# A twelve-sublayer decoder on one core: gathered cross-attention and a ternary feed-forward layer reordered

## The reference

```
x = x + L0_attn(norm(x));  x = x + L0_xattn(norm(x), ctx);  x = x + L0_ffn(norm(x))
x = x + L1_attn(norm(x));  x = x + L1_xattn(norm(x), ctx);  x = x + L1_ffn(norm(x))
x = x + L2_attn(norm(x));  x = x + L2_xattn(ctx, norm(x));  x = x + L2_ffn(norm(x))
x = x + L3_attn(norm(x));  x = x + L3_xattn(norm(x), ctx);  x = x + L3_ffn(norm(x))
```

```
L1_xattn:  Q, K, V = h Wq + bq, ctx Wk + bk, ctx Wv + bv        (16 heads of width 8)
           head i sees only the context rows i, i+16, i+32, ... (32 of 512)
           softmax(Q K^T / sqrt(8)) V, then Wo + bo
L3_ffn:    quant_weight(w): s = max(mean|w|, 1e-5);  clip(round(w / s), -1, 1) * s
           quant_act(x):    c = 127 / max(max|row|, 1e-5); clip(round(x c), -128, 127) / c
           g = gelu(quant_act(h) quant_weight(w1)^T)            (128 -> 512)
           quant_act(g) quant_weight(w2)^T                      (512 -> 128)
```

## Time and profile before

| | |
|---|---|
| three timed runs | 1631.58, 1636.93, 1637.21 us; median 1636.93 |
| profiled execution | 1631.73 us, span 1629.5 us, mean granted TensorE clock 0.859 |
| busy, share of the span | PE 76%, DVE 58%, ACT 42%, POOL 15% |
| L1_xattn, start of its norm to its last update of x | 460.8 to 534.05 us |
| L3_ffn, from h to its last update of x | 1564.9 to 1625.8 us |
| DMA | 114.55 MB, 70 GB/s over the span |

### The profile page before, as it was taken

How to read it: one execution, slowest core, us unless ns; L and a number is a source line. 1 busy time by engine, 2 the same in 40 slices (tenths; PEclk the granted TensorE clock), 3 DMA queues, 4 the chain that set the end, 5 groups by cost and what they waited for, 6 DMA issues and landing times. The chain is left out here.

```text
span 1629.5 us, 26020 instructions
## 1 busy us (share of the span) xinstructions
PE 1242.9 (76%) x9190; PEld 758.0 (47%) x9234; DVE 941.5 (58%) x2485; ACT 691.0 (42%) x1299; POOL 251.8 (15%) x525
## 2 busy tenths in 40 slices
PE   4777997784875487456999999999857689789922
PEld 1333434672331387234666666666547423323311
DVE  5558864335654444664676676767530555677666
ACT  2544872221622021101666666666424235446612
POOL 2211111451010254100000000000036112111100
PEclk8787998897896599767999999999968779989965
DMA  5425210784330366000000000000056331311000
GB/s 138 116 81 139 70 63 25 220 274 100 68 110 0 136 226 200 13 0 0 1 2 1 1 2 1 1 1 2 9 152 213 100 88 22 102 53 39 17 13 13
DMA packets 85553, 114.55 MB, mean 70 GB/s; under 512 B 11234, under 2 KB 65711, under 8 KB 85151
## 3 DMA queue, kind: packets, MB, share of 16 engines
q1 hardware_dynamic: 80978, 103.78, 21.8%
q0 software_dynamic: 4448, 9.12, 1.8%
HBM read 85.79 MB, written 26.61 MB: 69 GB/s over the span
## 5 line engine op out<-in xcount | busy, mean ns | idle before, releaser
L662 DVE TENSOR_REDUCE mx<-ps 128x4 f32<-128x1024 f32 (+1 forms) x128 | 153.7, 1222 | 72.0 <-PE ps L599 63.7
L805 PE MATMUL ps<-probs,vaug 128*32 128x256 f32 (+1 forms) x1792 | 145.8, 400 | 13.3 <-ACT probs L773 9.1
L2175 DVE CUSTOM_DVE_ANT_0 wring<-ps,probs 128x768 f32<-128x768 f32 x128 | 122.6, 958 | 56.9 <-PE ps L2047 56.8
L2131 ACT COPY qs<-ps 128x768 f32<-128x768 f32 x128 | 102.4, 801 | 97.6 <-PE ps L2054 97.6
L763 ACT ACTIVATE probs<-ps 128x1024 f32<-128x1024 f32 x96 | 98.3, 1024 | 86.1 <-PE ps L637 86.1
L768 ACT ACTIVATE probs<-ps 128x512 f32<-128x512 f32 x192 | 106.2, 594 | 51.3 <-PE ps L725 49.4
L2113 ACT ACTIVATE wring<-wring,r 128x768 f32<-128x768 f32 x128 | 120.7, 943 | 2.9 <-DVE r L2178 2.9
L236 POOL TENSOR_TENSOR rstd<-veps,mhalf 128x8 f32<-128x8 f32 x14 | 23.2, 1657 | 617.9 <-DVE veps L221 590.6
L599 PE MATMUL ps<-ks,qs 49*128 49x256 bf16 (+1 forms) x512 | 85.0, 374 | 39.6 <-DVE mx L657 12.0
L2054 PE MATMUL ps<-ident,wring 128*128 128x128 f32 x768 | 110.4, 281 | 3.2 <-DVE wring L2212 3.2
L2054 PEld LDWEIGHTS ps<-ident,wring 128*128 128x128 f32 x768 | 84.6, 141 | 39.4 <-issue 35.3
(11 more groups left out here) (313 smaller groups left out, 2352.4 us busy)
## 6 DMA issues: line engine op xcount, KB each, us to landing
wring<-in_L_ffn_w SPq DMA_DIRECT2D x19, 768.0 KB
wring<-in_L_ffn_w SPq DMA_DIRECT2D x32, 384.0 KB
wring<-in_L_ffn_w SPq DMA_DIRECT2D x19, 514.0 KB
scr_q<-probs SPq DMA_DIRECT2D x10, 384.0 KB, 3.4
scr_k<-probs SPq DMA_DIRECT2D x27, 128.0 KB, 4.2
qs<-scr_q SPq DMA_DIRECT2D x18, 192.0 KB
probs<-in_L_ffn_w SPq DMA_DIRECT2D x8, 384.0 KB
probs<-in_L_ffn_w SPq DMA_DIRECT2D x4, 768.0 KB
```

The lines of the kernel that those rows point to most:

```text
L662: dve.tensor_reduce(out, src, AX.X, ALU.max, negate=True).then_inc(a_max.sem, 1)
L805: ins = pe.matmul(ps[32 * j:32 * j + 32, self.av_bank(s), q0:S], vaug[:, s % 2, kt, j, :], probs[:, s % 2, j, at:at + S - q0], start=(kt = ...
L2131: act.copy(self.pT[:, g % 2, j, :, k * P:(k + 1) * P], self.buffer("turn", i, 0, KV).rearrange("p (t n) -> p t n", n=P)).then_inc(self.out ...
L2175: dve.tensor_tensor_reduce(self.sc[:, s, :], src, self.maskb[:, u // (2 * PR), :], 1.0, -3.0e38, ALU.add, ALU.max, self.top[:, s:s + 1]).t ...
```

## The change

In L1_xattn the context is loaded without a wait into the upper half of `qs`; PE makes the keys before the norm's transposes, in place of the dummy matmuls, and DVE masks two batches in the norm's hook and two after h. Queries come before values; the bias and mask of the values are applied after the scores of tile 1. `pr` has three buffers and `pT` two. PE issues score t+1 ahead of turn t-1, and the output products of a batch inside the loop, two batches behind. SP waits for the keys and values before it issues the six loads of L2_xattn.

In L3_ffn the weights are loaded at the start of L2_ffn, their magnitudes summed behind the copy of its block 5, the sum over partitions made at the start of L3_attn, the rounding done between L3_attn's projections and its loop. The scales of all 8 token tiles are computed together, the tiles quantised in two halves. ACT's Gelu reads PSUM and scales by a column, so L2346 is gone; the inner tiles are quantised in pairs with two slots, four products with w1 run ahead, and x is stored in four DMAs. ACT begins the sublayer with a Gelu of one column.

```diff
                     others[7].context_vector(dve, *divmod(b - 2, CTX_STEPS))
+                if m == 2 and b == 6:
+                    others[11].weights_vector(dve)
...
+        ctxg = qs[:, B * PAIRS * S + 1024:].bitcast(F32)[:, 0:TC]
+        pr = tmp[:, TC + 512 + T:TC + 2048 + T].rearrange("p (s n) -> p s n", s=3)
+        pT = tmp[:, TC + 2048 + T:TC + 2048 + 3 * T].rearrange("p (s c n) -> p s c n", s=2, c=NQ)
...
         def sync(self, sp):
-            sp.wait_ge(x_done.sem, x_done.at(self.sub - 1, 1))
             sp.dma_start(self.ctxg, a["ctxT_by_head"]).then_inc(g_ctx.sem, 16)
...
+        def context_tensor(self, pe):
             pe.wait_ge(g_ctx.sem, 16)
             for b in range(B):
                 pe.matmul(bank(b), wt("L1_xattn_k"), self.ctxg[:, b * S2:(b + 1) * S2],
                           start=True, stop=True).then_inc(g_k_mm.sem, 1)
+
+        def tensor(self, pe):
+            for c in range(2):
+                pe.wait_ge(ln_hT.sem, ln_hT.at(self.norm, c + 1))
+                pe.matmul(bank(5 + c), wt("L1_xattn_q"), hT[:, c * 512:c * 512 + 512],
+                          start=True, stop=True).then_inc(two_mm.sem, 1)
             for t in range(B * NQ):
                 c = t % NQ
                 ins = pe.matmul(bank(4, t * 32, t * 32 + 32), self.ctxg[:, t * P:(t + 1) * P],
                                 wt("L1_xattn_v")[:, c * 32:c * 32 + 32], start=True, stop=True)
             ins.then_inc(g_v_mm.sem, 1)
...
+            self.score_tensor(pe, 0)
+            for t in range(NT + 1):
+                if t + 1 < NT:
+                    self.score_tensor(pe, t + 1)
+                if t:
+                    self.turn_tensor(pe, t - 1)
+                if t and t % 2 == 0:
+                    self.sum_tensor(pe, t // 2 - 1)
+                if t >= 4 and t % 2 == 0:
+                    self.y_tensor(pe, t // 2 - 2)
+            self.y_tensor(pe, B - 1)
+
...
-                    act.activation(self.pr[:, t % 2, :], self.pr[:, t % 2, :], ACT.Exp).then_inc(tile_act.sem, 1)
+                    act.activation(self.pr[:, t % 3, :], self.pr[:, t % 3, :], ACT.Exp).then_inc(tile_act.sem, 1)
                 elif what == "turn":
                     act.wait_ge(tile_tp.sem, tile_tp.at(0, t + 1))
-                    if t >= 2 and t % 2 == 0:
-                        act.wait_ge(g_av.sem, g_av.at(0, t // 2))
...
+        def context_vector(self, dve):
+            self.keys_vector(dve, 0)
+            self.keys_vector(dve, 1)
+
+        def keys_vector(self, dve, b):
+            dve.wait_ge(g_k_mm.sem, g_k_mm.at(0, b + 1))
...
+            self.keys_vector(dve, 2)
+            self.keys_vector(dve, 3)
...
-                    if t >= 2:
-                        dve.wait_ge(tile_tp.sem, tile_tp.at(0, t - 1))
+                    if t >= 3:
+                        dve.wait_ge(tile_tp.sem, tile_tp.at(0, t - 2))
                     dve.tensor_tensor(pr, src, wide(top), ALU.subtract).then_inc(g_s_sub.sem, 1)
+                    if t == 1:
+                        self.values_vector(dve)
...
+        held = qs[:, B * PAIRS * S:].bitcast(F32)
...
         def sync(self, sp):
-            sp.wait_ge(x_done.sem, x_done.at(self.sub - 1, 1))
+            sp.wait_ge(x_done.sem, x_done.at(7, 1))
             sp.dma_start(self.w1, a["L3_ffn_w1"]).then_inc(f_in.sem, 16)
             sp.dma_start(self.w2, a["L3_ffn_w2"]).then_inc(f_in.sem, 16)
 
+        def out_sync(self, sp):
+            for p in range(NT // 2):
+                sp.wait_ge(f_done.sem, f_done.at(0, 2 * p + 2))
+                sp.dma_start(a["out"].rearrange("(t p) d -> p t d", p=P)[:, 2 * p:2 * p + 2, :],
+                             x[:, 2 * p:2 * p + 2, :]).then_inc(written, 16)
+
...
+        def weights_tensor(self, pe):
+
+            pe.wait_ge(f_abs.sem, f_abs.at(0, 1))
+            pe.matmul(bank(0, 0, 2), self.ones, self.col(0, 2), start=True, stop=True).then_inc(f_tot.sem, 1)
...
+            pe.wait_ge(f_wq.sem, f_wq.at(0, 2))
+            for t in range(4):
+                self.up_tensor(pe, t)
+            for p in range(NT // 2):
+                self.turn_tensor(pe, 2 * p)
+                self.turn_tensor(pe, 2 * p + 1)
+                if 2 * p + 4 < NT:
+                    self.up_tensor(pe, 2 * p + 4)
+                    self.up_tensor(pe, 2 * p + 5)
+                self.down_tensor(pe, 2 * p)
+                self.down_tensor(pe, 2 * p + 1)
+
...
+            act.activation(self.col(128), self.ones[:, 0:1], ACT.Gelu)
...
+            for t in range(4):
+                self.gelu_scalar(act, t)
+            for q in range(NT):
+                act.wait_ge(tile_tp.sem, tile_tp.at(1, q + 1))
+                if q >= 2:
+                    act.wait_ge(f_y.sem, f_y.at(0, q - 1))
+                act.copy(self.ziT[:, q % 2, :], bank(2 + q % 2).bitcast(BF16)[:, 0:FH]).then_inc(tile_T.sem, 1)
+                if q % 2 and q + 3 < NT:
+                    self.gelu_scalar(act, q + 3)
+                    self.gelu_scalar(act, q + 4)
+
+        def gelu_scalar(self, act, t):
+            act.wait_ge(f_h.sem, f_h.at(0, t + 1))
+            if t >= 4:
+                act.wait_ge(f_hq.sem, f_hq.at(0, t // 2 - 1))
+            act.activation(self.z[:, t // 2 % 2, t % 2, :], bank(self.h_bank[t % 4]), ACT.Gelu,
+                           scale=self.col(16 + t)).then_inc(tile_act.sem, 1)
+
...
+        def rounded_vector(self, dve):
+
             do = lambda ins: link(dve, dchain, ins)
...
+                do(dve.tensor_scalar(self.wtmp, wgt, self.col(4 + k), ROUND, ALU.mult, ALU.add))
                 do(dve.tensor_scalar(self.wtmp, self.wtmp, ROUND, 1.0, ALU.subtract, ALU.min))
                 dve.tensor_scalar(self.wint[:, k, :], self.wtmp, -1.0, None, ALU.max).then_inc(f_wq.sem, 1)
                 dve.wait_ge(f_wq.sem, f_wq.at(0, k + 1))
...
+        def scales_vector(self, dve, big, inv, scale, weight, n):
+
+            do = lambda ins: link(dve, dchain, ins)
+            do(dve.tensor_scalar(self.col(big, n), self.col(big, n), EPS, None, ALU.max))
+            do(dve.reciprocal(self.col(inv, n), self.col(big, n)))
+            do(dve.tensor_scalar(self.col(inv, n), self.col(inv, n), 127.0, None, ALU.mult))
+            do(dve.tensor_scalar(self.col(scale, n), self.col(big, n), 1.0 / 127.0, self.col(weight), ALU.mult, ALU.mult))
+
+        def hidden_vector(self, dve, p):
+            z, zi = self.z[:, p % 2, :, :], self.zi[:, p % 2, :, :]
+            dve.wait_ge(tile_act.sem, tile_act.at(1, 2 * p + 2))
+            link(dve, dchain, dve.tensor_reduce(self.col(48 + 2 * p, 2), z, AX.X, ALU.max, apply_absolute_value=True))
+            self.scales_vector(dve, 48 + 2 * p, 56 + 2 * p, 32 + 2 * p, 3, 2)
+            for t in range(2):
+                ins = dve.tensor_scalar(z[:, t, :], z[:, t, :], self.col(56 + 2 * p + t), ROUND, ALU.mult, ALU.add)
+            link(dve, dchain, ins)
+            if p >= 2:
+                dve.wait_ge(tile_tp.sem, tile_tp.at(1, 2 * p - 2))
+            dve.tensor_scalar(zi, z, ROUND, None, ALU.subtract).then_inc(f_hq.sem, 1)
+
...
+        def vector(self, dve):
+            dve.wait_ge(ln_h.sem, ln_h.at(made(self.norm), 1))
+            link(dve, dchain, dve.tensor_reduce(self.col(64, NT), h[:, :, :], AX.X, ALU.max, apply_absolute_value=True))
+            self.scales_vector(dve, 64, 72, 16, 2, NT)
+            for half in range(2):
+                tiles = range(4 * half, 4 * half + 4)
+                for t in tiles:
+                    ins = dve.tensor_scalar(h[:, t, :], h[:, t, :], self.col(72 + t), ROUND, ALU.mult, ALU.add)
+                link(dve, dchain, ins)
+                dve.tensor_scalar(self.hi[:, 4 * half:4 * half + 4, :], h[:, 4 * half:4 * half + 4, :], ROUND, None,
+                                  ALU.subtract).then_inc(f_q.sem, 1)
+            for p in range(NT // 2):
+                self.hidden_vector(dve, p)
+                if p:
+                    self.out_vector(dve, 2 * p - 2)
+                    self.out_vector(dve, 2 * p - 1)
+            self.out_vector(dve, NT - 2)
+            self.out_vector(dve, NT - 1)
...
+                if s == 8:
+                    others[11].sync(sp)
                 mixtures[s].sync(sp)
-            elif s in others and s != 7:
+            elif s in others and s not in (7, 11):
                 others[s].sync(sp)
                 if s == 4:
+                    sp.wait_ge(g_k_mm.sem, g_k_mm.at(0, B))
+                    sp.wait_ge(g_v_mm.sem, g_v_mm.at(0, 1))
                     others[7].sync(sp)
-        sp.wait_ge(x_done.sem, x_done.at(N_SUB_RUN - 1, 1))
-        sp.dma_start(a["out"].rearrange("(t p) d -> p t d", p=P), x[:, :, :]).then_inc(written, 16)
-        sp.wait_ge(written, 48)
+        others[11].out_sync(sp)
+        sp.wait_ge(written, 96)
...
-                norm_vector(dve, norm_of[s], meanwhile=subs[s].context_vector if s in subs and subs[s].cross else None)
```

(11 more changed lines are left out.)

249 lines of the change are left out of this document (98 added, 151 removed).

## The result

The changed kernel takes 1571.17 us (median of four runs, 1568.29 to 1576.57), the kernel before 1634.26 (median of four); the ratio is 0.9627, with a 95% interval of 0.9578 to 0.9676. The profiled execution took 1572.72 us, its span is 1570.6. The forecast was 1572.0 for that execution and 1575 for the median. So the total was hit closely, but terms of the sum missed in opposite ways, and the experiments are mostly about these.

What follows compares the result with a forecast made beforehand. Bound: the order of work in L1_xattn, DVE in L3_ffn. Savings 26.7 + 33.1 + 0.8 - 0.9 = 59.7 us gave 1572.0 for the profiled execution; 3 on top for the median made 1575, range 1567 to 1586.

Steps and rivals of the forecast that it cites:

- Part 1: L1_xattn's front: keys ahead of the norm and queries before values gain 4.1 us, first reduction at 475.3.
- Part 2: L1_xattn's loop, scores a tile ahead: sublayer ends at 507.3 instead of 534.05, gaining 26.7 us including the front.
- the walk through PE's queue: L1_xattn's loop: PE's steps behind an odd tile summed, giving a pair 8.8 us at the lower clock, 6.6 at full.
- I take 30% of the time at the lower: L1_xattn's loop and end: clock share chosen between 36.8 us (lower) and 30.0 (full); sublayer gain 26.7, between 22.0 and 28.8.
- Rival 1: L1_xattn's loop stays at the lower clock: 4.8 us more, 1580; chance 0.13.
- Rival 2: L1_xattn: scores ahead don't break the ring, ACT's or PE's order keeps pairs near 13.5 us: 1595; chance 0.05.
- Part 3: L3_ffn from h to the last update: 27.8 us instead of 60.9, 33.1 saved, DVE setting the pace.
- Rival 3: L3_ffn: the ring through PE and ACT sets the pace at 6 us a pair, not 4.4: 1581; chance 0.07.
- The stores: End of L3_ffn: output in four 128 KB stores instead of one saves 0.8 us, between -0.6 and 1.1.
- Costs elsewhere: Moved weight work: nothing in L2_ffn, 0.5 plus 0.4 us in L3_attn; bounds 0 and 3.
- The 0.5 for the tiny product on PE: L3_attn: a narrow product ahead of the dummy matmuls delays PE by 0.5 us, between 0 and 0.9.
- Rival 4: Slower than before: SP's new waits delay L2_xattn's six loads so DVE stands still in L1_ffn; chance 0.01.

Runs made afterwards that it cites:

- Experiment 3: Changed kernel with L1_xattn's key matmuls and masked copies behind the norm again: norm start to first reduction 17.25 us against 14.52; L1_xattn 49.7 us.
- experiments 1: Kernel before with only the change of L1_xattn, L3_ffn and its store as before: 1585.81 us, ratio 0.9824.
- 7: Changed kernel with both L3_ffn weights summed and rounded at the start of L3_ffn instead of earlier sublayers: L3_ffn 40.62 us instead of 35.46.
- 8: Changed kernel with the scale of each L3_ffn token tile worked out by itself: L3_ffn 43.64 us, 8.2 longer.
- 9: Changed kernel with one 512 KB store at the end instead of four: 3.7 us from last update of x to span end, against 2.26 to 2.37.
- 10: Changed kernel with the first three w1 products and their Gelus in L3_ffn ahead of the second four token tiles: L3_ffn 34.17 us, 1.3 less.
- experiment 4: Changed kernel with L1_xattn's scores of tile t+1 behind the transposes and sums of tile t-1 again: 1577.08 us, L1_xattn 71.31.
- the first and the third batch: First four and last four follow-up runs, on chips numbered 13 and 9; kernel before took 1612.69 and 1616.38 us there.
- the second batch: The middle four follow-up runs, on the chip numbered 13; kernel before took 1633.23 us there.

## Why the forecast was right, and where it was off

**Part 1.** Forecast 4.1, measured 4.05. The keys end 6.3 us behind the norm's start, not 5, and the transposes, which wait for h, hide that. Experiment 3 shows that the keys alone are worth 2.7 of it. So close a hit is in part luck: the forecast gave the front no spread by the clock, and with 14.3 to 15.8 us in eleven traces the gain was anywhere from 2.8 to 4.25.

**Part 2, the step that was mis-sized.** First reduction to the multiplication of tile 1: forecast 8.65, measured 8.6 to 9.0. Behind it the bounds of the walk through PE's queue hold up well, in eight traces with the same loop (the changed kernel twice, and experiments 1, 3, 7, 8, 9 and 10):

| stretch | forecast, full / lower | measured at clock 1.00 | measured lower (clock) |
|---|---|---|---|
| pair of tiles 2, 3 | 6.1 / 7.9 | 6.15 | 7.98 to 8.00 (0.50 to 0.67) |
| pair of tiles 4, 5 | 6.6 / 8.8 | 6.58 to 6.60 (one of them at 0.99) | 7.92 to 8.22 (0.78 to 0.79) |
| pair of tiles 6, 7 | 4.8 / 5.75 | 4.72 to 4.73 | 4.72 to 5.17 (0.67 to 0.73) |
| end | 3.8 / 5.65 | 4.01 to 4.02 | 4.52 to 5.72 (0.50 to 0.77) |
| loop and end | 30.0 / 36.8 | | 30.9 to 34.4, mean 33.2 (0.70 to 0.85) |

What failed is "I take 30% of the time at the lower": it made 32.0 us, and the profiled execution took 34.2, which by the same two ends is (34.2 - 30.0) / 6.8 = 62%. Nor does the time follow the share: the clock of 0.76 over loop and end means 48% at the lower level, and the pair of tiles 2 and 3 took 7.99 us at a clock of 0.50 and at 0.67 alike. In seven of the eight traces that pair met a low clock. So the sublayer saved 24.5 instead of 26.7, inside the 22.0 to 28.8 that I had given. Rival 1, the whole loop at the lower clock, didn't come: no trace shows it in all stretches. Nor is there one right share; the same loop gave 30.9 and 34.4 us. The Trainium skill (TensorE: Matmul & The Clock Gate, A second HAM failure mode) describes such swinging between half and full rate in groups of matmuls with small pauses; the traces agree that it swings, with 0.62, 0.79, 1.00 and 0.73 in four stretches that follow each other; that the pauses are the cause, no run here shows.

**Rival 2** (the ring isn't broken, 13.5 us a pair) fell, and experiment 4 shows that it would have been true for the other order.

**Part 3.** Forecast 27.8 us from h, measured 26.7, so 34.2 saved instead of 33.1. By steps: tokens quantised in 4.8 (5.15), first pair at 8.13 (8.5), a pair 3.65 (3.76), two updates 0.52 (0.65), the end 2.83 (2.95). Nearly every term was a little dear: the wide subtraction took 0.69 where I took 0.78 between 0.55 and 0.86, and four products 0.87 where I had 1.07. The wait ahead of the first pair came out at the 3.35 that I had added up, though the Gelus in it were dearer. What I misread is the loop before: I called DVE "nearly always at work" there, but 7.5 us of it were waits for PE's product with w2, one in each tile. The new order, in which the updates of a pair stand behind the next pair, has no wait there until the last two, 1.47 us. By the experiments 5.2 us of the 35.65 come from the moved weights (7), 8.2 from the gathered token tiles (8) and 1.4 from the stores (9). The other 20.9, the inner loop, rest on the timelines: no run takes its pairs, or the Gelu out of PSUM, back by itself. Rival 3 fell, as DVE has no idle time between the pairs. The Gelu with a column operand took 0.695 us, where the earlier trace rows had 0.63 from SBUF and the exponential at L768, which reads PSUM at the same width and without such an operand, 0.594. The group on ScalarE, and then the page's row of that exponential (busy us, mean ns):

```profile
L2366 ACT ACTIVATE probs<-ps,r 128x512 f32<-128x512 f32 x8 | 5.0, 695 | 0.7 <-PE ps L2323 0.7
```

```profile
L768 ACT ACTIVATE probs<-ps 128x512 f32<-128x512 f32 x192 | 106.2, 594 | 53.0 <-PE ps L725 51.1
```

So the difference is 0.10 here, of which the column is the likely but not the only possible cause, since the functions differ too. The Trainium skill (ScalarE: Activation LUTs, What ACT_TABLE_LOAD costs) gives 93 ns for a column; the traces agree with that.

**The stores** saved 1.4 us, not 0.8, and experiment 9 confirms it. I had forecast a tail of 2.8 us, from the 2.5 in which a 128 KB write landed; it was 2.3 us in all, with the issue in it, as SyncE's queue shows in the changed kernel (span end 1570.6):

```profile
1568.34 0.37 SPq L2285 DMA_DIRECT2D out<-x  x1
```

The Trainium skill (DMA: Bandwidth & Descriptors, Anatomy of one DMA) names some 2.0 us as the fixed part of a DMA. That section is about DMAs that GpSimd issues, and these stores are issued by SyncE; both tails measured here, 2.3 us for 128 KB and 3.7 for 512 KB, lie above it.

**Costs elsewhere.** I had put 0.9 on L3_attn. Its first maximum came 0.6 late, as worked out, but the third only 0.2, since another wait ends there. The 0.5 for the tiny product on PE didn't appear: behind the dummy matmuls PE now waits 1.35 us for h, where the earlier trace rows had 0.16. PE's timeline there:

```profile
1259.57 0.58 PE L2298 MATMUL ps<-r,qs 128*128 128x2 f32 x2 [7.28 <-DVEq L2550]
1260.01 4.71 PE L2580 MATMUL ps<-m3a,identb 128*128 128x512 bf16 x15
1266.08 1.09 PE L244 MATMUL ps<-ident,h 128*128 128x128 f32 x8 [1.35 <-DVE h L226]
```

The error was to take the 0.16 as a fixed margin. It goes with the clock of the dummies: they ended 6.35 us behind the norm's start at 0.54 in the kernel before, and 5.23 at 0.71 in the changed one. The transposes started 6.51 us behind the norm's start in the three traces without the product and 6.58 or 6.59 in the eleven with it, even in the one in which the dummies, at 0.55, ended no earlier than h. So product and means together cost 0.07 us there. L3_attn as a whole took 116.9 to 118.1 us in the three traces without the rounding and 117.4 to 118.7 in the eleven with it; what is left, some 0.5 us, is within its own spread. L2_ffn: nothing, as forecast. Rival 4 was far away: the six loads are issued from 472.39 to 477.14, and the first that reads them starts at 550.98. L1_ffn (122.99 and 123.10 us) and L2_xattn (419.35 and 419.49) didn't grow.

**The sum.** Against the profiled span before: 24.5 + 35.65 + 0.2 = 60.35 saved in the sublayers that I had costed at 59.7, and 1.4 us lost in all the others together, which leaves 58.9 (1629.5 to 1570.6). The loop's 2.2 us too few stand against 1.1 in L3_ffn, 0.6 in the stores and 1.1 in L3_attn. That the profiled execution came within 0.7 us of 1572.0 is luck: the misses cancel, and the first sublayer alone, which nothing touches, took from 110.6 to 117.4 us in the fourteen traces. The 3 us that I put on top for the median weren't needed; the median lies 1.5 below the profiled execution this time.

## What to carry to other kernels

Where two engines hand tiles to each other in a ring, look at what stands in the queue ahead of the operation that the other engine needs next: here putting that one first was worth over 20 us, and without it the further buffers gained nothing. Price such a loop at both clock levels and forecast the middle of them with the full width as its range (here 33.4 us, and eight traces had a mean of 33.2), unless the bound is an engine whose time didn't change with that clock. Before you call an engine the bound, add up its waits: DVE in L3_ffn looked always busy and waited 7.5 us. A vector instruction on one number per lane costs nearly what one on eight does (0.15 against 0.17 us here), so gather the scales of several tiles before you work on them.

## What was unexpected in the hardware

The same instructions of L1_xattn's loop and end took from 30.9 to 34.4 us in eight executions, and what differs in the rows is the granted clock of single stretches. L2_ffn took 99.3 to 102.0 us in the first and the third batch, and 110.4 to 113.1 in the second batch and the first comparison, with or without a change in it; the kernel before as a whole differed by some 20 us between them (1612.69 and 1616.38 against 1633.23 and 1634.26). Since the first two batches ran on the same chip number, it isn't shown that the chip makes the difference. The traces show one thing more: in the six long ones PE stands idle for 7.4 to 13.0 us of L2_ffn, most of it ahead of its matmuls at L1287 and L1300, and the profile names nothing that it waited for; in the eight short ones there is no such idle time. What held it wasn't tested. For a change worth a few us, this means that only runs of one batch may be compared, and that a sublayer's own length in the trace tells more than the total.
